# Linear attention on one core: an image's solution in three pieces, outputs nine chunks behind

## The reference

```python
qkv = x @ w_qkv.T                       # x: layernorm of h, per image 3136 x 192
q, k, v = ...                           # 12 heads of 16
q = q / max(sum over tokens |q|, 1e-12) # the same for k
kv  = einsum('bhnd,bhne->bhde', k, v)   # a 16 x 16 matrix for each head and image
out = einsum('bhnd,bhde->bhne', q, kv)
return out @ w_proj.T + b_proj
```

## Time and profile before

| | |
|---|---|
| median of 3 runs | 3054.92 us (3054.26 to 3055.03) |
| the profiled execution | 3053.52 us, span 3051.6 us |
| busy share of the span | PE 81%, DVE 70%, ACT 45%, POOL 31% |
| linear attention | from 2066.5 us; its last statistics end about 2581.5 us |

### The profile page before, as it was taken

How to read it: one execution, slowest core, us unless ns; L and a number is a source line. 1 busy time by engine, 2 the same in 40 slices (tenths; PEclk the granted TensorE clock), 3 DMA queues, 4 the chain that set the end, 5 groups by cost and what they waited for, 6 DMA issues and landing times. The chain is left out here.

```text
span 3051.6 us, 47169 instructions
## 1 busy us (share of the span) xinstructions
PE 2468.8 (81%) x14074; PEld 1780.3 (58%) x14075; DVE 2131.2 (70%) x5754; ACT 1382.0 (45%) x2332; POOL 955.0 (31%) x998
## 2 busy tenths in 40 slices
PE   8999999999979999956666399992677777667765
PEld 4444444444458888845555399992566666344443
DVE  6777777777558889865555344445777975899996
ACT  2444444444423333333333256653755742466665
POOL 0101001000000000036666344447866850333333
PEclk9999999999989999965555699995877878576666
DMA  1000000000000000032222577762111110000001
GB/s 51 0 17 12 8 19 1 8 1 0 1 8 0 0 0 0 0 117 73 72 71 73 167 248 257 258 233 73 50 39 39 51 30 20 13 23 21 23 23 28
DMA packets 67538, 162.25 MB, mean 53 GB/s; under 512 B 13009, under 2 KB 30646, under 8 KB 66878
## 3 DMA queue, kind: packets, MB, share of 16 engines
q1 hardware_dynamic: 37858, 94.18, 9.5%
q0 software_dynamic: 21504, 44.99, 5.2%
q10 hardware_dynamic: 8064, 21.68, 2.3%
HBM read 63.89 MB, written 63.88 MB: 42 GB/s over the span
## 5 line engine op out<-in xcount | busy, mean ns | idle before, releaser
L418 DVE TENSOR_REDUCE pmax<-ppre 112x1 f32<-112x512 f32 x656 | 424.4, 686 | 162.5 <-PE ppre L260 162.4
L211 ACT ACTIVATE prob<-pscore 128x896 f32<-128x896 f32 x336 | 308.1, 917 | 423.9 <-PE pscore L293 423.9
L307 PE MATMUL pout<-prob,xkey 128*64 128x448 f32 x1344 | 328.3, 567 | 0.4 <-ACT prob L211 0.4
L260 PE MATMUL ppre<-xh,yh 49*112 49x512 f32 x656 | 291.6, 447 | 7.8 <-DVE pmax L418 4.2
L260 PEld LDWEIGHTS ppre<-xh,yh 49*112 49x112 f32 x656 | 112.7, 172 | 239.8 <-issue 103.5
L1692 POOL DMA_INDIRECT yg<-rows_out,place x224 | 229.7, 1025 | 62.4 <-issue 62.2
L293 PE MATMUL pscore<-yh,xh 49*128 49x448 f32 x700 | 241.2, 422 | 0.4 <-DVE yh L438 0.4
L1112 POOL DMA_INDIRECT rows_in<-xn,idx x224 | 216.9, 968 | 66.1 <-issue 63.0
L2145 POOL TENSOR_TENSOR yg<-y,gout 112x512 f32<-112x512 f32 x112 | 141.1, 1270 | 275.9 <-DVE y L2369 275.9
L193 POOL CAST yh<-ynext 113x448 fp32r<-113x448 f32 x28 | 17.2, 614 | 667.8 <-DVE pmax L418 639.8
L1550 POOL TENSOR_TENSOR zl<-z,zh 128x448 fp32r<-128x448 f32 x126 | 144.5, 1146 | 211.6 <-ACT zh L1523 202.2
(11 more groups left out here) (376 smaller groups left out, 6652.3 us busy)
## 6 DMA issues: line engine op xcount, KB each, us to landing
wd<-down SPq DMA_DIRECT2D x63, 512.0 KB, 3.0
xb<-rows_in SPq DMA_DIRECT2D x63, 448.0 KB, 3.6
rows_out<-yb ACTq DMA_DIRECT2D x63, 336.0 KB, 3.2
out<-ho SPq DMA_DIRECT2D x28, 336.0 KB, 2.9
rows_in<-zero SPq DMA_DIRECT2D x15, 448.0 KB
rows_in<-xn,idx POOLq DMA_INDIRECT x224
yg<-rows_out,place POOLq DMA_INDIRECT x224
xkey<-in_xkey SPq DMA_DIRECT2D x4, 800.0 KB, 6.5
```

Source lines behind the costliest of these rows:

```text
L211: nc.scalar.activation(prob[j % 3][:, :, :], pscore[j % 2][:, :, 0:CH], ACT.Exp).then_inc(exped, 1)
L260: pe.matmul(out[:, :], yh1[rows, q * T:(q + 1) * T], xh[b % 2][rows, block * 512:(block + 1) * 512], start=True, stop=True, tile_position= ...
L307: mm = pe.matmul(pout[i * LO:(i + 1) * LO, 0:CH], xkey[b % 2][:, 2 * j + i, :], prob[j % 3][:, i, :], start=(j == 0), stop=(i == 1 and j = ...
L418: nc.vector.reduce_max(pmax[:, q, 2 * block + half:2 * block + half + 1], bank(u, depth), AX.X).then_inc(pre_max, 1)
```

## The change

The solution of image b - 1 is cut in pieces inside the next image's first three chunks. Its products now all go to pqk[1] (two halves side by side), since pg already gathers the next image's Gram matrix. The order in chunk 0 is, on TensorE: transposes, turn_gram, gram, keys_map; chunk 1: values_map ahead of the transposes, project_map behind gram; chunk 2: image_map ahead of the transposes. VectorE's parts: gram_turned behind low and keys_mapped behind add_experts (chunk 0), values_mapped ahead of low and map_projected behind add_experts (chunk 1), image_mapped ahead of low (chunk 2). values_map and image_map wait for the key sum of the chunk before (b_sum), and the key product waits for the copy out of pqk[1]. Outputs of chunk n are mapped and added in step n + 9 (LATE), with transposed rows in a ring of ten slots (RING); sums is doubled. After the loop the last image's solution runs with two of the remaining nine mappings between its parts, and seven behind it.

```diff
+    LATE = CPI + 2
+    RING = LATE + 1
-        xTA = sb("xTA4", [128, TOK])
-        xTB = sb("xTB4", [RB + 1, TOK])
+        xTA = sb("xTA4", [128, RING, CH])
+        xTB = sb("xTB4", [RB + 1, RING, CH])
-        sums = sb("sums4", [128, 3, CPI])
+        sums = [sb(f"sums4_{i}", [128, 3, CPI]) for i in range(2)]
...
+            def gram(g, b, c):
+                if c == 0 and b:
+                    pe.wait_ge(S["g_out"], b)
...
                     elif m == 1 and g:
                         pe.wait_ge(S["b_sum"], g)
+                        if b and c <= 2:
+                            pe.wait_ge(S[("t2_out", "m1_out", "wi_out")[c]], b)
...
+            def turn_gram(b):
                 pe.wait_ge(S["g_out"], b + 1)
                 pe.wait_ge(S["b_sum"], CPI * (b + 1))
+                pe.transpose(pqk[1][:, 0:128], gsb[:, 0, D - 128:D], eye[:]).then_inc(S["gt_mm"], 1)
+            def values_map(b):
                 pe.wait_ge(S["t2_out"], b + 1)
+                if b + 1 < B:
+                    pe.wait_ge(S["b_sum"], CPI * (b + 1) + 1)
...
+            def image_map(b):
                 pe.wait_ge(S["m1_out"], b + 1)
+                if b + 1 < B:
+                    pe.wait_ge(S["b_sum"], CPI * (b + 1) + 2)
...
+            for s in range(NC):
+                b, c = divmod(s, CPI)
+                if b and c == 1:
+                    values_map(b - 1)
+                if b and c == 2:
+                    image_map(b - 1)
+                transposes(s)
+                if b and c == 0:
+                    turn_gram(b - 1)
+                gram(s, b, c)
+                if b and c == 0:
+                    keys_map(b - 1)
+                if b and c == 1:
+                    project_map(b - 1)
+                if s >= LATE:
+                    map_out(s - LATE)
+                if s == 0:
+                    pe.wait_ge(S["split"], 4)
+                q_and_k(s, b, c)
+            turn_gram(B - 1)
+            map_out(NC - LATE)
+            keys_map(B - 1)
+            map_out(NC - LATE + 1)
+            values_map(B - 1)
+            project_map(B - 1)
+            image_map(B - 1)
+            for n in range(NC - LATE + 2, NC):
+                map_out(n)
...
+            def copies(g):
+                if g >= RING:
+                    act.wait_ge(S["o_mm"], 2 * (g - RING) + 2)
...
                         act.wait_ge(S["g_mm"], CPI * (b + 1))
+                        if b:
+                            act.wait_ge(S["t2_mm"], b)
...
             for s in range(-3, NC):
                 b, c = divmod(s, CPI)
+                if s >= CPI and c == 1:
+                    values_mapped(b - 1)
+                if s >= CPI and c == 2:
+                    image_mapped(b - 1)
                 if s >= 0:
                     low(s)
+                if s >= CPI and c == 0:
+                    gram_turned(b - 1)
                 if here(s + 2):
                     offset(s + 2)
                 if here(s + 3):
                     add_experts(s + 3)
+                if s >= CPI and c == 0:
+                    keys_mapped(b - 1)
+                if s >= CPI and c == 1:
+                    map_projected(b - 1)
                 if here(s + 2):
                     add_moe(s + 2)
-                if s >= CPI:
-                    add_out(b - 1, c)
+                if s >= LATE:
+                    add_out(s - LATE)
...
```

More of the change, by code:

```diff
@@ L1663, in linear_attention_phase @@
         NW = 5
-        PAIRS = TPI // 2
         LEAD = 4
@@ L1727, in _, with transposes @@
             pe.wait_ge(S["w_ready"], 4)
-            def gather(g, c):
+            def transposes(g):
                 pe.wait_ge(S["xn_ready"], g + 1)
@@ L1788, in solve @@
                     for c, k in enumerate(ROWS4):
-                        mm = pe.matmul(pqk[i][0:ROWS4[i], 0:D], gsb[0:k, c, COLS[i]], wT[0:k, c, D:2 * D],
-                                       start=(c == 0), stop=(c == 1))
+                        mm = pe.matmul(two(i, D), gsb[0:k, c, COLS[i]], wT[0:k, c, D:2 * D],
+                                       start=(c == 0), stop=(c == 1), skip_group_check=True)
                 mm.then_inc(S["t2_mm"], 1)
+            def values_map(b):
                 pe.wait_ge(S["t2_out"], b + 1)
+                if b + 1 < B:
+                    pe.wait_ge(S["b_sum"], CPI * (b + 1) + 1)
                 for i in range(2):
@@ L1795, in solve, with project_map @@
                         v = slice(2 * D + COLS[i].start, 2 * D + COLS[i].stop)
[L1796 to L1797 removed]
+                        mm = pe.matmul(two(i, ROWS4[i]), wT[0:k, c, v], t2[0:k, c, COLS[i]],
+                                       start=(c == 0), stop=(c == 1), skip_group_check=True)
                 mm.then_inc(S["kv_mm"], 1)
+            def project_map(b):
@@ L1799, in solve @@
                 pe.wait_ge(S["kv_out"], b + 1)
                 for i, k in enumerate(ROWS4):
-                    mm = pe.matmul(pqk[i][0:k, 0:D], kvT[i][:], wpT[0:k, i, :], start=True, stop=True)
+                    mm = pe.matmul(two(i, D), kvT[i][:], wpT[0:k, i, :], start=True, stop=True, skip_group_check=True)
                 mm.then_inc(S["m1_mm"], 1)
+            def image_map(b):
                 pe.wait_ge(S["m1_out"], b + 1)
+                if b + 1 < B:
+                    pe.wait_ge(S["b_sum"], CPI * (b + 1) + 2)
@@ L1883, in _ @@
                 if s >= 0:
-                    copies(s, c, b)
+                    copies(s)
                     magnitudes(s, c, 0)
@@ L1959, in stats_of, with add_out @@
                     nc.vector.bn_stats(bns[:, t + q, :], h[:, t + q, :])
-            def add_out(b, c):
+            def add_out(n):
                 for r in range(2):
[L1963 to L1967, removed]
+                    p = 2 * n + r
+                    if p:
+                        dve.wait_ge(S["h_out"], p + 2)
+                    dve.wait_ge(S["o_mm"], p + 1)
+                    two = h[:, 2 * p:2 * p + 2, :]
@@ new lines, in two, with link, gram_turned @@
+            def two(i, cols):
+                return pqk[1][0:ROWS4[i], i * D:i * D + cols]
+            links = [0]
+            def link(ins):
+                links[0] = links[0] + 1
+                ins.then_inc(S["dvec"], 1)
+                dve.wait_ge(S["dvec"], links[0])
+            def gram_turned(b):
+                dve.wait_ge(S["gt_mm"], b + 1)
+                nc.vector.tensor_copy(gsb[0:RB, 1, 0:128], pqk[1][128 - RB:128, 0:128]).then_inc(S["gt_out"], 1)
+                dve.wait_ge(S["a_sum"], 2 * CPI * (b + 1))
+                dve.wait_ge(S["b_sum"], CPI * (b + 1))
+                link(nc.vector.tensor_reduce(nrm[:], sums[b % 2][:], AX.X, ALU.add))
@@ L2047, in _ @@
                     dve.wait_ge(S["qk_mm"], 3 * s + 2)
-                    nc.vector.tensor_reduce(sums[:, 1, c:c + 1], pqk[1][:, 0:CH], AX.X, ALU.add,
+                    nc.vector.tensor_reduce(sums[b % 2][:, 1, c:c + 1], pqk[1][:, 0:CH], AX.X, ALU.add,
                                             apply_absolute_value=True).then_inc(S["b_sum"], 1)
-                if s >= 0 and c == CPI - 1:
-                    if b:
-                        last_stats(b - 1)
-                    solve(b)
-            for c in range(CPI):
-                add_out(B - 1, c)
-            last_stats(B - 1)
+            gram_turned(B - 1)
+            add_out(NC - LATE)
+            keys_mapped(B - 1)
+            add_out(NC - LATE + 1)
+            values_mapped(B - 1)
+            map_projected(B - 1)
+            image_mapped(B - 1)
+            for n in range(NC - LATE + 2, NC):
+                add_out(n)
+            dve.wait_ge(S["h_out"], 2 * NC + 2)
+            stats_of(NT - 2)
 def bit_ffn_phase(nc, ins, h, bns, mean, rstd, var, eye, out):
```

65 lines of the change are left out of this document (27 added, 38 removed).

## The result

| | before | after |
|---|---|---|
| median of 4 runs | 3054.98 us | 3036.01 us (3032.32 to 3038.39) |
| ratio | | 0.9937 (95%: 0.992 to 0.9954) |
| the profiled execution, its span | 3053.52, 3051.6 us | 3034.65, 3032.7 us |
| linear attention in it | 515.3 us | 496.5 us |

The kernel is 19.0 us faster; 16.2 were forecast (3038.7, range 3026 to 3045). The last row of the table is measured from VectorE's first instruction of the phase (minus, 2066.52 before and 2066.10 after) to the first of the next (mean, 2581.78 and 2562.62). It differs by 18.7 us, so the whole difference lies in this phase.

What follows compares the result with a forecast made beforehand. GpSimd sets the pace; VectorE's lateness at xl beyond its slack is kernel time. -52.4 + 32.0 + 1.2 + 3.0 = -16.2 us, against the median 3054.9 gives 3038.7 us; 8 in 10 range 3026 to 3045.

Steps and rivals of the forecast that it cites:

- Removed: Ends of images 0, 1 and 2: the serial solution and GpSimd's waits for it go, -52.4 us.
- Chunk 0: Next image's first chunk: VectorE's added 1.94 us, less slack, loses 0.25 in image 1, 0.9 each in images 2 and 3.
- Cost nothing: Chunk 0: the turn needs the key sum, but VectorE spends that time in low, so no loss.
- Chunk 1: values_map, ahead of the transposes, waits for the key sum: 4.0 us lost in image 1, 4.9 each in images 2, 3.
- Chunk 2: image_map, ahead of the transposes, makes VectorE 6.4 us late: 5.4 lost in each of images 1 to 3.
- Sum given back: Chunks 0 to 2 of images 1 to 3: 32.0 us of the 52.4 lost again, nothing from chunk 3 on.
- The ones row: Memset ahead of the first gather: the ring's row grows from seven to ten chunks, +1.2 us.
- The end: After the loop: two mappings inside the last image's serial solution delay it, +3.0 us, bounds -0.5 and +4.
- Higher clock at the handoffs: Rival: chunk 1 late by 3.4 instead of 5.1, chunk 2 by 4.0 instead of 6.4; 3024 us, chance 0.10.
- TensorE becomes the bound: Rival: waits keep TensorE at 0.50 in an image's first three chunks, kernel slower, 3075 us; chance 0.04.
- All hidden: Rival: handoffs cost VectorE no more than its slack, GpSimd goes on at 13.85; 3007 us, chance 0.05.
- faster: Whole kernel: faster by over 0.2% (6 us), chance 0.94.

Runs made afterwards that it cites:

- serial_late: Changed kernel with the solution back at each image's end, late outputs and ring kept, two copies of wimg: 3054.92 us, ratio to before 1.0004.
- turn_behind: Changed kernel with turn_gram behind the Gram products instead of ahead of them in chunk 0: 3031.61 us, ratio 0.992.
- after_again: The changed kernel run and profiled once more, without an edit: 3037.12 us, ratio 0.9934.
- busy_short: Changed kernel with unread products on TensorE, 10 ahead of turn_gram, 6 each ahead of values_map and image_map: 3032.74 us, ratio 0.9928.
- end_straight: Changed kernel with the two mappings of image 2 ahead of the last solution instead of inside it: 3044.25 us, ratio 0.9965.
- rows_first: Changed kernel with transposes ahead of values_map and image_map, and VectorE's copies of the two behind low: 3030.21 us, ratio 0.9918.
- behind_gram: Changed kernel with every solution piece behind the Gram products, VectorE's copies behind add_experts, map_projected behind add_moe: 3026.67 us, ratio 0.9911.
- early_copies: behind_gram with first product group and project_map ahead of mapping (chunks 1, 2), values_mapped and image_mapped behind offset, map_projected ahead of add_moe: 3017.1 us, ratio 0.9875.

## Why the prediction was right, step by step

- **Removed, -52.4: right.** Shown by serial_late, whose own three ends hold 48.4. By the key sums those of the kernel before held 52.1.
- **Chunk 0, +0.25, +0.9, +0.9: too small.** Measured +1.0, +3.9, +2.0. "Cost nothing" for the turn was the failed step: it delays VectorE by nothing, but holds the Gram products behind it on TensorE, which then start late, at the lower clock, and take 4.37 us where I had 3.79. keys_map's wait, which I took at none with 0.8 as bound, was 1.06. turn_behind removes all of it down to 1.0.
- **Chunk 1, +4.0, +4.9, +4.9: the mechanism right, the size too large.** Measured +2.5, +3.8, +3.0. The premise that TensorE would be at 0.50 at every handoff failed here: in images 2 and 3 chunk 0's late line keeps it busy until the key sum, and in image 1 it was at the higher level in spite of 2.67 us of waiting (in after_again, in the same place, at the lower one). Where turn_behind takes that line away, the lateness is the 5.1 of the prediction (4.8 in image 3). Chunk 0 and chunk 1 are two errors of opposite sign, in images 2 and 3 with one cause.
- **Chunk 2, +5.4 each: right.** Measured +5.5, +5.5, +5.2, with VectorE's waits of 3.76 and 2.01 in image 2. That TensorE is at the lower clock here depends on chunk 1: in turn_behind and busy_short it was not in three places, and the loss was 3.2.
- **Sum given back, 32.0: measured 32.5**, chunk 3 of images 1 and 2 (+0.4, -0.2) included. That the sum agrees so closely is luck: chunk 0 cost 4.9 us more than forecast and chunk 1 4.6 less.
- **The ones row, +1.2: right.** From minus to the first gather it took 3.74 us before and 4.86 after; the memset is now 3.83.
- **The end, +3.0: too large.** Measured +0.4 in the profiled run, +2.0 in the second profile (15.8 and 17.4 against 15.4); counted to the end of the phase -0.1 and +1.3. I had added the mappings to a solution at the lower clock; in the first they kept the clock up, so that keys_map, values_map and image_map all ran at the higher one. The lower bound, -0.5, had that case. end_straight shows that they hide well: ahead of the solution they cost 4 to 6 more. This is the largest error that nothing cancelled, and it is about as large as the 2.7 us by which the median missed the forecast.
- The terms give -52.1 + 32.5 + 1.1 + 0.4 = -18.1 of the 18.7 measured. Counted by the key sums nothing is left over: +0.8 up to the first, -52.1 and +32.5, +0.2 because chunks 0 and 1 of image 1 run at 13.97, without a mapping, and -0.1 behind the last.
- **The rivals.** "Higher clock at the handoffs" (3024) had its prices right, 3.4 at chunk 1 (measured 3.4 in two images of three) and 4.0 at chunk 2 (4.05 in turn_behind), and its chance too low: in the two profiles of the changed kernel it came true at five of six handoffs in chunk 1 and at none of six in chunk 2. That chunk 0 cost more hid this in the total. "TensorE becomes the bound" did not decide, but it is the 2.07 us ahead of one key sum, and it is what limits the repairs (rows_first, behind_gram) until the order on TensorE is changed too. Its price was too high: the 12.1 us a chunk divide by seven a stretch of the earlier trace rows that holds the next solution's first 16 us as well (11.34 of its 84.87 us busy); without it they are 10.5. "All hidden" (3007) is not reached by early_copies either (3017).

The median stands 2.7 us under the forecast, and one profile differs from the other by 4.8 us in this phase. The bounds of my own range were added up wrongly: they give 3028 to 3042, not 3030 to 3043. The chance that I gave to "faster" rests on serial_late's term being so large beside all others; that part was safe.

## What to carry to other kernels

A piece of work that is spread into another loop's steps costs little by its own instructions and much by its place in each queue: put it behind whatever the other engines wait for next, and ask of each wait not only whom it delays but what stands behind it on its own engine. When one such hold-up is taken away, the next queue's order becomes the limit, so the order is to be moved on all engines together, and judged over the following chunks, not the one edited. Where TensorE is waited for in short bursts, two profiles of one kernel differ, and not only where the edit is; compare chunk by chunk, over all chunks and over several runs.

## What the runs showed of the hardware

- **TensorE stayed at 0.50 through 15 us of gapless work** (the changed kernel, 2359 to 2374: 14.93 of 15.00 us busy), and in turn_behind through 19 us with 18.40 busy (2338 to 2357). In an ordinary chunk of the kernel before it began at 0.50 at 2255.30 and stood at 1.00 from 2262 to 2268. The "within 5 us" of my prediction left out what came before: from 2217.7 to 2236, solution and first chunk, TensorE was at 0.50 with 15.4 of 18.3 us busy. The Trainium skill (TensorE: Matmul & The Clock Gate, "What's actually happening") has sustained activity release the throttle; these stretches do not agree, and I don't know what set them apart.
- **GpSimd's small instructions stretch under VectorE's large ones.** The power of four values for each of 112 rows (L1704) took 1.04, 1.65 or 2.93 us, and the sum (L1700) 0.20 or 1.93, in one kernel. GpSimd's timeline in chunks 0 and 1 of image 2 of early_copies, and VectorE's product and two adds of add_moe in chunk 0, with its rows that wait for GpSimd at the end of both chunks:

```profile
2327.93 2.93 POOL L1704 TENSOR_TENSOR rst<-veps,mhalf 112x4 f32<-112x4 f32 x1
...
2333.61 1.05 POOL L1713 TENSOR_TENSOR rst<-veps,mhalf 112x4 f32<-112x4 f32 x1
...
2342.57 1.93 POOL L1700 TENSOR_TENSOR veps<-agg,eps 112x4 f32<-112x4 f32 x1
```
```profile
2328.14 0.94 DVE L1975 TENSOR_TENSOR yf<-yf,gam 112x768 f32<-112x768 f32 x1
2329.01 0.94 DVE L1977 TENSOR_TENSOR h<-h,bet 112x768 f32<-112x768 f32 x1
2329.99 0.96 DVE L1980 TENSOR_TENSOR h<-h,yf 112x768 f32<-112x768 f32 x1
...
2334.69 0.16 DVE L1993 SCALAR_TENSOR_TENSOR off<-agg,rst 112x4 f32<-112x4 f32 x1 [0.21 <-POOL rst L1713]
...
2350.17 0.16 DVE L1993 SCALAR_TENSOR_TENSOR off<-agg,rst 112x4 f32<-112x4 f32 x1 [1.20 <-POOL rst L1713]
```

The power ends at 2330.86, with the third of them (2330.95). The Trainium skill (SBUF — State Buffer, "Who interferes with whom") says that a VectorE instruction with two SBUF inputs contends with a GpSimd instruction that reads SBUF; these rows agree, all three being of that kind. So part of the 1.0 us that chunk 0 loses even in the best versions is GpSimd held up, not VectorE late: GpSimd shows almost no wait there. An estimate of how much comes from VectorE's waits for GpSimd's power, 0.21 and 1.20 us: without them it would have taken 14.7 and 14.3 us for the two chunks, so 0.8 and 0.4 of the 1.0 and 1.6 lost are its own length beyond the pace, and the rest is in GpSimd's line alone. No run removes the one without the other.
- **One cast came late.** In chunk 1 of image 2 of the changed kernel the cast to xh starts 1.76 us after the start of transposes that took 0.99; in images 1 and 3 it starts 1.02 after, and behind transposes at the lower clock 1.79. The profile names no releaser, and the cause stays open. It is why the higher clock was worth only 0.9 us at that one handoff.
